# Feed-forward weights turned by the host: VectorE adds the raw tile to the low-rank product, ScalarE and GpSimd split it later

## The chip, the cores and the metric

The kernel runs on one core of a Trainium2 chip. The core has TensorE (PE in the rows), VectorE (DVE), ScalarE (ACT), GpSimd (POOL) and SyncE (SP), which issues the DMAs here. The metric is device microseconds of one execution. Three runs of the kernel before gave 982.81, 984.64 and 989.12 us; the median is 984.64 us.

## The reference

A layer on x of 2 x 1024 tokens of 512 features. LayerNorm of x feeds a causal attention with 32 heads of size 16 and 8 key groups, and a feed-forward block whose three weights each carry a low-rank term of rank 16. The result is x plus the product of the two:

```python
xn = _layernorm(x, axis=-1)
s = _L0_attn_ref(xn, Wq, Wkv, Wo, bo)
gate = xn @ gate_w.T + (xn @ gate_a.T) @ gate_b.T          # gate_w: 1376 x 512, gate_a: 16 x 512
up   = xn @ up_w.T   + (xn @ up_a.T)   @ up_b.T
hidden = silu(gate) * up
g = silu(hidden @ down_w.T + (hidden @ down_a.T) @ down_b.T)
return x + s * g
```

The kernel adds the low-rank product to the weight first (w + b a), once for each tile of 128 of the 1376 hidden features, and then multiplies.

## The kernel before

All float32 products are made of rounded parts: a tile is split in hi (ScalarE rounds it to float32r) and lo (the difference), and three matmuls hi·hi, hi·lo and lo·hi are summed in PSUM. So each weight tile goes through "fold" (sum of the weight and the low-rank product), "hi" and "lo" before its first use.

Two programs are interleaved on every engine. The **attention** walks through 640 slots: 16 rounds (batch x key group) of 40 slots, one head and key job in each. At even slots TensorE issues a pair of transposed score matmuls (`st`, two PSUM banks, one for each head); ScalarE makes `prob = exp(st)`, one head per slot. The next `st` pair waits until both exponentials of the pair before are done. TensorE also issues pairs of plain scores (`s`, three banks), which VectorE reduces to maxima (`part_max`), and every few slots the context matmuls (`o<-prob,v`) after GpSimd has masked the diagonal blocks. The maxima of half a round are negated, split (`neg_pad`, VectorE), transposed (`s<-ident,neg_pad`) and copied out (`neg_rows`, ScalarE).

The **background** is everything else, counted in steps (`STEPS`), and `interleave` gives about one step to each slot. Each engine has its own copy of the background, in which the same yields stand, so that an operation placed after some number of steps lands in a known slot. In order: LayerNorm and transposes of x, projections (`proj`), values, then for each of the NH = 11 tiles h of hidden features `hidden(h, c)` for four token chunks c of 8 steps each, one `proj` of 4 steps after c = 1, and the two folds (gate and up, 2 steps each) of tile h+1 also after c = 1. One h takes 40 steps, so a round. Then 11 down folds of 2 steps each, then `down(t)` and `out(t)` for 16 token tiles. The folds of tile 0 stand after the projection `AFTER[0]`, at the start of the attention; the down folds stand in slots 483 to 503, well before the attention's end.

A fold before: four TensorE transposes of the raw 128 x 512 tile (L909), four low-rank matmuls into the same bank (L913), ScalarE rounds the bank to `w_hi` (L1157), VectorE subtracts from the bank to get `w_lo` (L1392). A down fold: four transposes (L948), one low-rank matmul of 512 columns (L952), ScalarE `down_hi` (L1176), VectorE `down_lo` (L1412). The raw tiles come by DMA (L646) into `ring`, eight tiles of 2 KB per partition. `low_a`, the rounded factor a, is made once: ScalarE rounds it (L1144) after the values are stored, VectorE subtracts its lo rows (L1380), and both wait in line with what follows on their engine. GpSimd works on `hid` (L512, L514, L520) and on the masks (L503) in this phase.

## Time and profile before

| | us |
|---|---|
| runs: median (lowest, highest) | 984.64 (982.81, 989.12) |
| the profiled execution's own time | 989.02 |
| its span, first to last instruction | 987.3 |
| mean granted TensorE clock | 0.977 |
| PE, DVE, ACT, POOL busy | 927.0, 576.7, 487.5, 318.1 |

The profile is of one execution. An engine's busy share averages over stages with different limits, so a stretch has to be looked at by itself: which wait ends last there. In a timeline, PE rows with xN merge N matmuls; the start of the next row shows what a group really took, since matmuls overlap in the pipeline. "PEclk" 1.00 is 2.4 GHz and 0.50 is 1.2 GHz.

### The profile page before, as it was taken

How to read it: one execution, taken by the hardware profiler on the slowest of the kernel's cores; microseconds unless marked ns; L12 is line 12 of the kernel's file. 1: busy time of each engine (PE TensorE's matmuls, PEld its weight loads, DVE VectorE, ACT ScalarE, POOL GpSimd, SP SyncE). 2: the span in 40 equal slices, each digit the busy share in tenths (PEclk: the TensorE clock that was granted, in tenths of full speed). 3: DMA queues.
4: the chain of work that ended last, by engine and by line, in shares of the span. 5: the costliest groups of instructions: out<-in, count | busy, mean ns of one | idle time of the engine just before them, and what ended most of it. 6: DMA issues, size and time to landing. Idle time of an engine off the chain costs nothing.

```text
span 987.3 us, 18068 instructions
## 1 busy us (share of the span) xinstructions
PE 927.0 (94%) x6599; PEld 598.5 (61%) x6599; DVE 576.7 (58%) x1659; ACT 487.5 (49%) x978; POOL 318.1 (32%) x320
## 2 busy tenths in 40 slices
PE   2797999999999999999999999999999999999986
PEld 2665667676766676767676766554555555555764
DVE  6755666666666666666666666676566656530025
ACT  2432556565656565656565656555444434435211
POOL 4022234343535352525252525330213122120126
PEclk9899999999999999999999999989999999999998
DMA  9456242424242424242424243367565454534454
GB/s 293 132 186 206 64 136 80 133 83 134 82 134 83 133 83 125 86 124 88 119 89 124 93 127 101 101 186 195 166 169 146 124 158 122 139 105 135 144 150 150
DMA packets 142934, 129.02 MB, mean 131 GB/s; under 512 B 36176, under 2 KB 104368, under 8 KB 142624
## 3 DMA queue, kind: packets, MB, share of 16 engines
q1 hardware_dynamic: 142848, 127.87, 43.6%
q8 instruction: 54, 0.88, 0.4%
q14 instruction: 32, 0.26, 0.1%
HBM read 74.07 MB, written 53.22 MB: 129 GB/s over the span
## 4 chain that ended last, share of the span: by engine, by line
PE 84%; DVE 8%; ACT 3%; DMA 2%; issue 2%; POOL 0%; SPq 0%; POOLq 0%; DVEq 0%; ACTq 0%
PE bank L934 24%; PE o L1071 12%; PE bank L246 9%; PE s L1035 9%; PE st L1054 9%; PE bank L247 7%; PE bank L248 7%; DVE junk L1516 2%; PE bank L896 2%; DVE neg_pad L1532 1%; PE bank L909 1%; PE bank L913 1%; DVE hid L1406 1%; DMA inv_sums<-scratch_r 1%; ACT gate L1168 1%
## 5 line engine op out<-in xcount | busy, mean ns | idle before, releaser
L1297 ACT ACTIVATE prob<-st 128x512 f32<-128x512 f32 (+1 forms) x640 | 324.3, 554 | 287.7 <-PE st L1054 287.1
L1516 DVE CUSTOM_DVE_ANT_0 junk<-s,mask 128x128 bf16<-128x128 f32 (+3 forms) x512 | 229.3, 487 | 116.3 <-PE s L1035 115.5
L1519 DVE TENSOR_REDUCE part_max<-s 128x1 f32<-128x512 f32 x256 | 163.8, 681 | 103.9 <-PE s L1035 103.7
L503 POOL TENSOR_SCALAR_AFFINE_SELECT prob<-prob 128x512 f32<-128x512 f32 x128 | 82.3, 655 | 262.1 <-ACT prob L1297 261.6
L1035 PE MATMUL s<-k,q 64*128 64x512 f32 (+3 forms) x768 | 150.0, 379 | 10.5 <-DVE part_max L1516 8.5
L934 PE MATMUL bank<-x_hi,w_hi 64*128 64x512 f32 (+1 forms) x704 | 150.9, 415 | 2.4 <-DVE hid L1406 1.1
L1071 PE MATMUL o<-prob,v 128*32 128x512 f32 (+3 forms) x1536 | 145.3, 497 | 0.0
L934 PE MATMUL bank<-x_lo,w_hi 64*128 64x512 f32 (+1 forms) x704 | 142.9, 391 | 0.0
L934 PE MATMUL bank<-x_hi,w_lo 64*128 64x512 f32 (+1 forms) x704 | 142.2, 389 | 0.0
L1054 PE MATMUL st<-q,k 64*128 64x512 f32 (+3 forms) x768 | 137.2, 375 | 3.9 <-ACT prob L1297 3.8
L512 POOL TENSOR_TENSOR tanh<-tanh,hid 128x512 f32<-128x512 f32 (+1 forms) x44 | 56.5, 1285 | 166.4 <-DVE hid L1406 166.4
L1035 PEld LDWEIGHTS s<-k,q 64*128 64x128 f32 x768 | 77.3, 186 | 52.6 <-DVE part_max L1516 28.3
L1054 PEld LDWEIGHTS st<-q,k 64*128 64x128 f32 x768 | 72.0, 185 | 59.6 <-issue 35.5
L934 PEld LDWEIGHTS bank<-x_hi,w_hi 64*128 64x128 f32 (+1 forms) x704 | 68.7, 182 | 41.3 <-issue 30.6
L246 PE MATMUL bank<-down_hi,hid_in 128*128 128x512 f32 (+1 forms) x176 | 79.2, 450 | 3.0 <-issue 2.3
L520 POOL TENSOR_TENSOR hid_lo<-hid,tanh_hid_hi 128x512 fp32r<-128x512 f32 (+1 forms) x44 | 56.7, 1288 | 75.9 <-ACT tanh_hid_hi L1185 75.9
L1071 PEld LDWEIGHTS o<-prob,v 128*32 128x32 f32 x1536 | 39.7, 110 | 66.2 <-issue 62.3
L934 PEld LDWEIGHTS bank<-x_lo,w_hi 64*128 64x128 f32 (+1 forms) x704 | 69.0, 182 | 12.6
L934 PEld LDWEIGHTS bank<-x_hi,w_lo 64*128 64x128 f32 (+1 forms) x704 | 69.1, 183 | 7.4
L247 PE MATMUL bank<-down_lo,hid_in 128*128 128x512 f32 (+1 forms) x176 | 70.1, 399 | 0.0
L248 PE MATMUL bank<-down_hi,hid_in 128*128 128x512 f32 (+1 forms) x176 | 69.9, 397 | 0.0
L514 POOL TENSOR_TENSOR hid<-tanh,hid 128x512 f32<-128x512 f32 (+1 forms) x44 | 56.5, 1283 | 3.5
(121 smaller groups left out, 1014.6 us busy)
## 6 DMA issues: line engine op xcount, KB each, us to landing
hid_in<-scratch_hid SPq DMA_DIRECT2D x16, 1408.0 KB, 7.4
q<-scratch_q SPq DMA_DIRECT2D x60, 200.0 KB
scratch_hid<-tanh_hid_hi SPq DMA_DIRECT2D x40, 256.0 KB, 2.1
scratch_hid<-hid_lo SPq DMA_DIRECT2D x40, 256.0 KB, 2.4
scratch_o<-o_sb SPq DMA_DIRECT2D x32, 256.0 KB
scratch_q<-proj_hi SPq DMA_DIRECT2D x30, 256.0 KB
k<-scratch_k SPq DMA_DIRECT2D x30, 192.0 KB
ctx<-scratch_o SPq DMA_DIRECT2D x16, 256.0 KB, 3.9
```

Of the source, the lines that this page charges most:

```text
L246: pe.matmul(out, lhs_hi, rhs_hi, start=start, stop=False)
L247: pe.matmul(out, lhs_hi, rhs_lo, start=False, stop=False)
L248: return pe.matmul(out, lhs_lo, rhs_hi, start=False, stop=stop)
L503: ins = pool.affine_select(out=blk, in_=blk, compare_op=ALU.is_ge, fill=0.0, base=0, pattern=[[0, REP], [1, P]], channel_multiplier=-1)
L520: pool.tensor_tensor(hid_l[0:hp, n % 2], hid[0:hp, n % 2], hid_h[0:hp, n % 2], ALU.subtract)\
L934: mm = pe.matmul(bank[i][0:hp, :], w_[half, h % 2, i, kt, 0:hp], x_[half, c, kt], start=not cross and kt == 0 and w_ is wh and x_ is xh, s ...
L1035: pe.matmul(sb_[(p + odd) % S_BANKS][:, 0:wd], q[half, g % 2, h // 2, qt * P:(qt + 1) * P], k[half, g % 2, k0:k0 + wd], start=True, stop=T ...
L1054: mm = pe.matmul(st[odd][:, col:col + q1 - q0], k[half, i % 2, kt * P:(kt + 1) * P], q[half, i % 2, h // 2, q0:q1], start=True, stop=True)
L1071: mm = pe.matmul(ob[32 * h:32 * h + 2 * HD, q0 % C:q0 % C + q1 - q0], v[:, i % 3, kt].rearrange("p a e -> p (a e)"), prob[:, job % 3, h, c ...
L1297: nc.scalar.activation(prob[:, job % 3, h, 0:JOB_COLS[j]], st[at % ST_BANKS][:, 0:JOB_COLS[j]], ACT.Exp, scale=float(HD) ** -0.5).then_inc ...
L1516: ins = dve.tensor_tensor_reduce(junk[:, n % S_BANKS, 0:wd], bank_[:, 0:wd], mask[:, C - wd:C], 1.0, LOWEST, ALU.add, ALU.max, part[:, h, ...
L1519: ins = dve.tensor_reduce(part[:, h, qt, dst:dst + 1], bank_[:, 0:wd], AX.X, ALU.max)
```

## The change

The host lays gate_w and up_w out transposed, in tiles [h, p, k, 128] of 128 hidden features, and down_w transposed, so a raw tile lands in the form in which the product needs it. The transposes on TensorE go. The sum is made by VectorE: `ring = bank + ring` (PSUM and SBUF in, SBUF out). ScalarE rounds the sum from `ring` to `w_hi` or `down_hi`, and GpSimd subtracts (`w_lo`, `down_lo`) from `ring`. A fold keeps its 2 steps. The folds of tile 0 move ahead of `AFTER[0]`. Raw tiles are reloaded after GpSimd's subtraction, later in the order. `down(0)` waits for each `down_lo` when it needs it.

```diff
+    for i in range(2):
+        yield "fold", 0, i
     for c, blk in AFTER[:SOON]:
         yield "proj", c, blk
-    for i in range(2):
-        yield "fold", 0, i
...
-                        fold=(w_lo, 2 * a + b + 1), down_fold=(d_lo, a + 1), down=(y_done, a + 1),
+                        fold=(w_sum, 2 * a + b + 1), down_fold=(d_sum, a + 1), down=(y_done, a + 1),
...
+            def low_weight(h, i):
+                n = 2 * h + i
+                pool.wait_ge(w_hi, n + 1)
+                pool.tensor_tensor(wl[:, h % 2, i, :, 0:rows[h]], raw_tile(n), wh[:, h % 2, i, :, 0:rows[h]],
+                                   ALU.subtract).then_inc(w_lo, 1)
+
+            def low_down(h):
+                hp = rows[h]
+                pool.wait_ge(d_hi, h + 1)
+                if h == NH - 1:
+                    pool.wait_ge(d_lo, h)
+                pool.tensor_tensor(dl[0:hp, h], ring[0:hp, (RAW_DOWN + h) % 8], dh[0:hp, h], ALU.subtract).then_inc(d_lo, 1)
...
             def fold(h, i):
-                pe.wait_ge(raw_landed[n % 8], DMA * (n // 8 + 1))
                 pe.wait_ge(low_lo, 2)
                 out_ = take_bank(("fold", h, i))
                 for kt in range(KT):
-                    pe.matmul(out_[:, kt * P:kt * P + hp], ring[0:hp, n % 8, kt * P:(kt + 1) * P], ident[0:hp, 0:hp],
-                              is_transpose=True, start=kt == 0, stop=False, skip_group_check=True)
-                yield 1
-                for kt in range(KT):
                     mm = pe.matmul(out_[:, kt * P:kt * P + hp], a_gu[:, i, kt * P:(kt + 1) * P],
-                                   bT[:, i, h * P:h * P + hp], start=False, stop=kt == KT - 1, skip_group_check=True)
-                mm.then_inc(filled, 1)
-                yield 1
+                                   bT[:, i, h * P:h * P + hp], start=True, stop=True)
+                    if kt == KT - 1:
+                        mm.then_inc(filled, 1)
+                    if kt % 2:
+                        yield 1
...
             def split_down(h):
-                key = ("down_fold", h, 0)
-                wait_filled(act, key)
-                nc.scalar.activation(dh[0:rows[h], h], bank_of(key)[0:rows[h], :], ACT.Copy).then_inc(d_hi, 1)
+                hp = rows[h]
+                act.wait_ge(d_sum, h + 1)
+                nc.scalar.activation(dh[0:hp, h], ring[0:hp, (RAW_DOWN + h) % 8], ACT.Copy).then_inc(d_hi, 1)
...
+                yield 1
                 for h in range(NH):
                     yield STEPS["down_fold"]
                     split_down(h)
...
+            def add_down(h):
+                key, hp, n = ("down_fold", h, 0), rows[h], RAW_DOWN + h
+                dve.wait_ge(raw_landed[n % 8], DMA * (n // 8 + 1))
+                wait_filled(dve, key)
+                dve.tensor_tensor(ring[0:hp, n % 8], bank_of(key)[0:hp, :], ring[0:hp, n % 8], ALU.add).then_inc(d_sum, 1)
```

How it moves instructions, at three places. First TensorE at the folds of tile 1, in round 1 (`bank<-bT,low_a` is the low-rank product, `bank<-ident,ring` the transposes). Before:

```order
L909 MATMUL bank<-ident,ring 128x128 x3
L1035 MATMUL s<-k,q 128x512 [waits s_read]
L1035 MATMUL s<-k,q 128x512
L913 MATMUL bank<-bT,low_a 128x128 x4
L1054 MATMUL st<-q,k 128x512 [waits exp_done]
L1054 MATMUL st<-q,k 128x512
L1035 MATMUL s<-k,q 128x384 [waits s_read]
L1035 MATMUL s<-k,q 128x384
```

and now:

```order
L940 MATMUL bank<-bT,low_a 128x128 [waits up_read,gate_read,low_lo_done]
L940 MATMUL bank<-bT,low_a 128x128
L1057 MATMUL s<-k,q 128x512 [waits s_read]
L1057 MATMUL s<-k,q 128x512
L940 MATMUL bank<-bT,low_a 128x128 x2
L1076 MATMUL st<-q,k 128x512 [waits exp_done]
L1076 MATMUL st<-q,k 128x512
L1057 MATMUL s<-k,q 128x384 [waits s_read]
L1057 MATMUL s<-k,q 128x384
```

The transposes are gone, and of the four products two now stand ahead of the `s` pair and two behind it; `st` and `s` stand where they did.

Second, ScalarE at the start of the attention, just behind the rounding of `low_a`. Before:

```order
L1144 ACTIVATE low_a<-prob 96x1024 [waits xn_ready,v_stored1,v_stored0]
L1297 ACT_TABLE_LOAD [waits p_stored1,p_stored0]
L1297 ACTIVATE prob<-st 128x512 [waits st_done] x2
L1125 ACTIVATE proj_hi<-bank 128x512 [waits p_stored0,filled]
L1297 ACTIVATE prob<-st 128x512 [waits st_done] x2
```

and now:

```order
L1166 ACTIVATE low_a<-prob 96x1024 [waits xn_ready,v_stored1,v_stored0]
L1178 ACTIVATE w_hi<-ring 128x512 [waits w_sum]
L1319 ACT_TABLE_LOAD [waits p_stored1,p_stored0]
L1319 ACTIVATE prob<-st 128x512 [waits st_done] x2
L1178 ACTIVATE w_hi<-ring 128x512 [waits w_sum]
L1319 ACTIVATE prob<-st 128x512 [waits st_done] x2
```

The first `w_hi`, which waits for VectorE's first sum, now stands ahead of the table load and the first exponentials. On TensorE the first fold stands where the projection's first six matmuls stood, and waits for `low_lo`, the lo rows of `low_a`.

Third, ScalarE at the first down folds. Before (the two `prob` rows behind each `down_hi` are the two heads of one `st` pair):

```order
L1314 ACTIVATE o_sb<-o 128x512 [waits o_stored1,pv_done]
L1176 ACTIVATE down_hi<-bank 128x512 [waits filled]
L1297 ACTIVATE prob<-st 128x512 [waits pv_done,st_done]
L1297 ACTIVATE prob<-st 128x512 [waits st_done]
L1176 ACTIVATE down_hi<-bank 128x512 [waits filled]
L1185 ACTIVATE tanh_hid_hi<-hid 96x512 [waits hid_done]
```

and now:

```order
L1336 ACTIVATE o_sb<-o 128x512 [waits o_stored1,pv_done]
L1319 ACTIVATE prob<-st 128x512 [waits pv_done,st_done]
L1195 ACTIVATE down_hi<-ring 128x512 [waits d_sum]
L1204 ACTIVATE tanh_hid_hi<-hid 96x512 [waits hid_done]
L1319 ACTIVATE prob<-st 128x512 [waits st_done] x2
L1327 ACTIVATE neg_rows<-s 32x128 [waits m_landed1,m_turned]
```

`down_hi` has moved from ahead of a pair of exponentials to between its two halves, and waits for VectorE's sum. (In the last `x2` row, the first is the second head of the pair above, the second the first head of the next pair.) All eleven down folds stand so now.

## Rows read from the trace of the kernel before

**Rows 1.** The page, parts 1 and 4: busy time, the chain by engine

```profile
PE 927.0 (94%) x6599; PEld 598.5 (61%) x6599; DVE 576.7 (58%) x1659; ACT 487.5 (49%) x978; POOL 318.1 (32%) x320
...
PE 84%; DVE 8%; ACT 3%; DMA 2%; issue 2%; POOL 0%; SPq 0%; POOLq 0%; DVEq 0%; ACTq 0%
```

**Rows 2.** Windows: stretch and length; busy us (instructions) of PE, PEld, DVE, ACT, POOL; PEclk, DMA share, GB/s

```profile
230.00:560.00 330.00, 326.76 (x2761) 218.96 (x2761) 205.64 (x632) 191.04 (x391) 135.11 (x135) 1.00 0.36 108
...
660.00:665.00 5.00, 5.00 (x19) 2.72 (x17) 3.00 (x15) 2.28 (x4) 0.63 (x1) 0.50 0.89 296
```

**Rows 3.** Timeline, folds of tile 3: start us, us, engine, line, operation [idle before, releaser]

```profile
226.65 0.50 PE L1054 MATMUL st<-q,k 64*128 64x512 f32 x2
226.76 0.60 ACT L1157 ACTIVATE w_hi<-bank 128x512 fp32r<-128x512 f32 x1 [1.74 <-PE bank L913]
...
227.25 1.08 ACT L1297 ACTIVATE prob<-st 128x512 f32<-128x512 f32 x2
227.38 0.66 PE L909 MATMUL bank<-ident,ring 128*128 128x128 f32 x4
...
227.79 0.64 PE L913 MATMUL bank<-bT,low_a 96*128 96x128 f32 x4
228.00 0.55 DVE L1516 CUSTOM_DVE_ANT_0 junk<-s,mask 128x384 bf16<-128x384 f32 x1
228.39 0.50 PE L1054 MATMUL st<-q,k 64*128 64x512 f32 x2
```

**Rows 4.** Groups by line and form: busy us, mean ns of one, idle before

```profile
L909 PE MATMUL bank<-ident,ring 128*128 128x128 f32 x80 | 13.4, 291 | 0.0
...
L948 PE MATMUL bank<-ident,ring 128*128 128x128 f32 x40 | 7.6, 319 | 0.6 <-DVE hid L1406 0.6
...
L520 POOL TENSOR_TENSOR hid_lo<-hid,tanh_hid_hi 128x512 fp32r<-128x512 f32 x40 | 51.6, 1289 | 66.4 <-ACT tanh_hid_hi L1185 66.4
...
L1392 DVE TENSOR_TENSOR w_lo<-bank,w_hi 128x512 fp32r<-128x512 f32 x20 | 13.8, 691 | 1.3 <-ACT w_hi L1157 0.7
```

**Rows 5.** Timeline, the start of the attention

```profile
88.78 0.50 PE L246 MATMUL bank<-x_hi,wq_hi 128*128 128x512 f32 x1
...
90.35 0.50 PE L1054 MATMUL st<-q,k 64*128 64x512 f32 x2
...
93.51 1.06 ACT L1144 ACTIVATE low_a<-prob 96x1024 fp32r<-96x1024 f32 x1 [4.40 <-DMA scratch_v<-v_sb]
94.58 1.28 ACT L1297 ACT_TABLE_LOAD   x1
94.60 1.22 DVE L1380 TENSOR_TENSOR low_a<-prob,low_a 32x1024 fp32r<-32x1024 f32 x1 [5.88 <-ACT low_a L1144]
...
95.88 1.08 ACT L1297 ACTIVATE prob<-st 128x512 f32<-128x512 f32 x2
...
96.56 0.80 PE L1035 MATMUL s<-k,q 64*128 64x512 f32 x2 [5.71 <-DVE part_max L1516]
...
100.14 0.79 PE L1054 MATMUL st<-q,k 64*128 64x512 f32 x2
```

**Rows 6.** Timeline, the same start, the first hidden product's weight load (PEld)

```profile
106.02 0.18 PEld L934 LDWEIGHTS bank<-x_hi,w_hi 64*128 64x128 f32 x2 [0.84 <-DVE w_lo L1392]
```

**Rows 7.** Timeline, the down folds

```profile
650.77 0.50 PE L1054 MATMUL st<-q,k 64*128 64x384 f32 x4
...
651.34 1.27 POOL L514 TENSOR_TENSOR hid<-tanh,hid 96x512 f32<-96x512 f32 x1
651.37 1.08 ACT L1297 ACTIVATE prob<-st 128x512 f32<-128x512 f32 x2
651.51 1.13 DVE L1532 TENSOR_TENSOR neg_pad<-neg_max,neg_pad 128x16 fp32r<-128x16 f32 x1
...
652.50 0.50 PE L1054 MATMUL st<-q,k 64*128 64x384 f32 x4 [0.41 <-ACT prob L1297]
```

**Rows 8.** Line 1532 (ns min/median/max; first and last start us)

```profile
L1532 DVE TENSOR_TENSOR neg_pad<-neg_max,neg_pad x32: 174/176/1157, 63.4 to 876.1; 128x16 fp32r<-128x16 f32 x32
```

More of the change, by code:

```diff
@@ L550, in background @@
                 low_query_weights(3)
+                yield NUMBER_STEPS["fold", 0, 1] - done
+                done = NUMBER_STEPS["fold", 0, 1]
+                for i in range(2):
+                    low_weight(0, i)
                 for h in range(NH):
@@ L560, in background @@
                         finish(h, c)
-                yield 2 * STEPS["down_fold"]
+                        if c == 1 and h + 1 < NH:
+                            yield 3 * STEPS["fold"]
+                            low_weight(h + 1, 0)
+                            yield STEPS["proj"] - STEPS["fold"]
+                            low_weight(h + 1, 1)
+                            done += 2 * STEPS["fold"] + STEPS["proj"]
+                yield 4
+                low_down(0)
                 low_hidden(NH - 1, NCH - 1)
-                yield (NH - 2) * STEPS["down_fold"]
+                for h in range(1, NH):
+                    yield STEPS["down_fold"]
+                    low_down(h)
                 def add(t):
@@ L635, in load_raw @@
                 elif before >= 0:
-                    wait_filled(sp, ("fold", *divmod(before, 2)))
+                    sp.wait_ge(w_lo, before + 1)
                 if n < RAW_LOW:
                     h, i = divmod(n, 2)
-                    dst, src = ring[0:rows[h], n % 8], raw_weights[i][h * P:h * P + rows[h]]
+                    dst, src = raw_tile(n), raw_weights[i][h, :, :, 0:rows[h]]
                 elif n < RAW_DOWN:
@@ L715, in background @@
                     store_value(c)
+                yield 2 * STEPS["fold"]
                 for c, blk in AFTER[:SOON]:
@@ L718, in background @@
                     store_projection(c, blk)
-                for i in range(2):
-                    yield STEPS["fold"]
-                    load_more_raw(i)
                 for h in range(NH):
@@ L728, in background @@
                             load_more_raw(RAW_LOW + c)
+                        if h == 0 and c == 0 or h + 1 < NH and c == 2:
+                            for i in range(2):
+                                load_more_raw(2 * (h + c // 2) + i)
                         if c == 1:
-                            if h + 1 < NH:
-                                for i in range(2):
-                                    yield STEPS["fold"]
-                                    load_more_raw(2 * (h + 1) + i)
-                            yield STEPS["proj"]
+                            yield (2 * STEPS["fold"] if h + 1 < NH else 0) + STEPS["proj"]
                             store_projection(*AFTER[SOON + h])
@@ L993, in background @@
                     yield from value(c)
+                for i in range(2):
+                    yield from fold(0, i)
                 for c, blk in AFTER[:SOON]:
                     yield from project(c, blk)
-                for i in range(2):
-                    yield from fold(0, i)
                 for h in range(NH):
@@ L1153, in split_weight @@
             def split_weight(h, i):
-                key = ("fold", h, i)
-                hp = rows[h]
-                wait_filled(act, key)
-                nc.scalar.activation(wh[:, h % 2, i, :, 0:hp],
-                                     bank_of(key)[:, :].rearrange("p (k h) -> p k h", k=KT)[:, :, 0:hp],
-                                     ACT.Copy).then_inc(w_hi, 1)
+                n = 2 * h + i
+                act.wait_ge(w_sum, n + 1)
+                nc.scalar.activation(wh[:, h % 2, i, :, 0:rows[h]], raw_tile(n), ACT.Copy).then_inc(w_hi, 1)
             def read_gate(h, c):
@@ L1239, in background @@
                 split_low_a()
+                for i in range(2):
+                    yield STEPS["fold"]
+                    split_weight(0, i)
                 for c, blk in AFTER[:SOON]:
@@ L1242, in background @@
                     split_projection(c, blk)
-                for i in range(2):
-                    yield STEPS["fold"]
-                    split_weight(0, i)
                 for h in range(NH):
@@ L1463, in background @@
                 low_of_low(1, a_gu, a_raw, slice(BESIDE_ROWS, 2 * BESIDE_ROWS))
+                for i in range(2):
+                    yield STEPS["fold"]
+                    add_weight(0, i)
                 for c, blk in AFTER[:SOON]:
@@ L1466, in background @@
                     low_projection(c, blk)
-                for i in range(2):
-                    yield STEPS["fold"]
-                    low_weight(0, i)
                 for h in range(NH):
```

71 lines of the change are left out of this document (34 added, 37 removed).

## The prediction

> **What bounds the kernel now.** I read the page first. TensorE is busy 94% of the span, and the chain that ended last runs on it for 84% [rows 1]: look for the engine that is both fullest and on the chain. The windows then say where that holds: from 230 to 560 us TensorE is busy 326.76 of 330 us at the full clock, 2.4 GHz [rows 2]. So work taken from TensorE can shorten this kernel, if the next engine has room at the very place where the work is taken. The rest of my reading is of timelines at those places: the ten pairs of gate and up folds in the steady rounds (all alike, one in each round; [rows 3] show one), the folds of tile 0 at the start [rows 5, 6], and the eleven down folds [rows 7].
>
> **Removed from TensorE.** In one fold the transposes start at 227.38 and the low-rank products at 227.79: four transposes cost 0.41 us on the path, not the 0.66 us of the row [rows 3], which overlap. Twenty folds in the steady rounds: 20 x 0.41 = 8.2 us. Eleven down folds: 11 x 0.41 = 4.5 us at the full clock, and more where the clock stood at 0.50, 1.2 GHz, as it did from 660 to 665 us [rows 2]; the mean of L948 is 319 ns against 291 of L909 [rows 4]. I take 5.0 us. The folds of tile 0: about 1 us. Full credit: some 14 us. What follows asks how much of it the other engines let through.
>
> **Steady rounds, ten places.** First half: the transposes ahead of the `s` pair go and half the products move behind it, so `s` comes only 0.2 us sooner and the `st` pair of 226.65 0.41 us sooner. Second half: from `st` at 226.65 to `st` at 228.39 are 1.74 us, of which TensorE would now need 1.74 - 0.41 = 1.33. But `st` at 228.39 needs both exponentials of the pair before, and these ended at 227.25 + 1.08 = 228.33 [rows 3]. TensorE and ScalarE tie here. The matmul takes 0.50, the two exponentials 1.08 and the handover 0.06, so the interval can't fall under 1.64 us: at most 0.10 is gained of the second 0.41. `w_hi` leaves its place ahead of these exponentials, which is what makes even that 0.10 possible. VectorE then holds the next `s` pair: it needs the bank of the first maximum of 384 columns, at 228.00 + 0.55 [rows 3], which stands in an unbroken row of VectorE work that starts from the `s` pair between the first fold's two parts and so moves by 0.2 to 0.3 us only. TensorE issues in order, so that is what the whole round gains. I take 0.3 us for each place, **-3.0 us** in all; the ends are 0.2 (VectorE moves with `s` alone) and 0.5 (0.41 + 0.10).
>
> What hides the added work: GpSimd's subtraction costs 1.29 us by its twin L520 [rows 4]; the first use of the tile is some 14 slots on, so it lies beside the products of c = 2 and 3, and GpSimd's next masks are four slots behind the first subtraction. VectorE's sum replaces L1392, 0.69 us, and no longer waits for ScalarE. ScalarE's rounding stays one operation of about 0.6 us, now ahead of two pairs in which TensorE has a projection to do. These cost nothing here; without that cover GpSimd would bring 20 x 1.29 = 26 us. The reloads of raw tiles, later on SP's queue, are four tiles of h ahead and not felt.
>
> **Start, tile 0.** Before, TensorE did six matmuls of the projection and an `st` pair (88.78 to 90.35 + 0.50) ahead of its 5.71 us wait, and ScalarE loaded its table (1.28) while VectorE made the lo rows of `low_a`, done at 94.60 + 1.22 = 95.82; the first exponentials ran at 95.88 [rows 5]. Now TensorE's first fold waits for those lo rows, so the 2.1 us of work ahead of the wait moves behind it. And ScalarE's first `w_hi` waits for VectorE's first sum: lo rows 95.82, two maxima of 384 columns to about 96.95 (0.55 each [rows 3]), sum 0.69 [rows 4], `w_hi` 0.60, then the table load 1.28, exponentials at 99.5 instead of 95.88. They end at 100.6, and the second `st` pair follows at about 100.7, where it stood at 100.14 [rows 5], but with the whole projection (12 matmuls of 0.26, by 88.78 to 90.35: 3.1 us) still to do in place of the folds (four parts of 0.41 to 0.66, about 2.2 us) and a wait of 0.84 us for `w_lo` [rows 6]. To the first hidden product, at 106.02 before, 5.9 us behind that `st` pair: 100.7 + 5.9 - 3.0 + 3.1 = 106.7 at the full clock. TensorE has two idle gaps instead of one, though, and after the one gap its matmuls ran at the lower level (0.79 us for an `st` pair at 100.14 against 0.50 at 90.35 [rows 5]), so part of the projection will take up to twice as long. I take **+1.5 us**, between 0 and +3.
>
> **Down folds.** Credit 5.0 us, as above. Against it stands ScalarE's order: `down_hi` sits between the two exponentials of each of the eleven pairs and waits for the sum. The chain of a pair becomes 0.50 (`st`) + 0.54 + 0.60 (`down_hi`) + 0.54 + 0.06 = 2.24 us, where the pair of 650.77 took 1.73 and already waited 0.41 us for the exponential [rows 7]. So 0.5 us more wherever TensorE has less to do than that; where a group of context matmuls stands in the pair, nothing. I count five such pairs besides the first: 2.5 us. The first pair is worse. VectorE's `neg_pad`, 0.176 us in the median [rows 8], took 1.13 at 651.51, until GpSimd's L514 ended at 652.61 [rows 7], and the first sum is next in VectorE's line: 652.64 + 0.69 = 653.3, then `down_hi` 0.6, `tanh_hid_hi` 0.6, second exponential 0.6: 655.1, where `st` stood at 652.50. That is 2.6 us, with all of TensorE's line behind it. Sum: -5.0 + 2.5 + 2.6 = **+0.1 us**. The ends: -5 (ScalarE never late) and +6 (0.5 on all ten other pairs, 2.6, and some 3 us of matmuls slowed by a lower clock that lasts through the stretch, less the credit and rounded). The four `wo_hi` behind it also sit in mid-pair: 2.24 us of chain against about as much TensorE work (six matmuls of 0.26 and two pairs of scores at about 0.35): +0.3. GpSimd's eleven `down_lo` take 14.2 us of a stretch of 30; `down(0)` waits for them one by one and is not held by the last of them.
>
> **Sum.** -3.0 + 1.5 + 0.1 + 0.3 = -1.1 us against the profiled execution's 989.02 (span 987.3 and 1.7 around it), so 987.9. That execution was 4.4 us above the median of the three, 984.64; off the median the forecast is **983.5 us**.
>
> **A rule weighed.** GpSimd held up VectorE's `neg_pad`, which reads two SBUF tiles (1.13 us against 0.176 [rows 7, 8]), yet L1392, which reads PSUM and SBUF, has a mean of 691 ns, that of the other VectorE operations on 512 columns, and was not held up [rows 4]. The Trainium skill, SBUF — State Buffer, section "Who interferes with whom", says that a VectorE instruction with two SBUF inputs and a GpSimd instruction that reads SBUF exclude each other for their whole length. By that rule the new sums (one PSUM input) are safe but 42 us more of GpSimd subtraction are added that can lock others out; the trace agrees on both kinds.
>
> **Rivals.**
> - *Full credit* (chance 0.12): ScalarE and VectorE overlap more than I read and TensorE's 14 us come off whole: 984.6 - 14 = 971. For it: TensorE is 99% busy in the rounds. Against: `st` at 228.39 came 0.06 us behind the exponentials [rows 3].
> - *Only the ends are better than I think* (0.10): the down folds give their 5, the start nothing: 984.6 - 3 - 5 = 976.5.
> - *GpSimd locks out VectorE* (0.10): the two `neg_pad`, the casts ahead of them and the four `wo_lo` near the down folds read SBUF alone; half of the eight meet a subtraction and lose 1.0 us each, the excess of 651.51 [rows 7, 8]: 983.5 + 4 = 987.5. Against it: the subtractions in the rounds stand at slots where no `neg_pad` is.
> - *Slower* (0.11): ScalarE's wait for the sum in mid-pair. One mechanism: sum late behind maxima, `down_hi` late, second exponential late, `st` late, `s` late, maxima late again, in all eleven pairs. By the first pair's loss, 2.6 us, on six of eleven and 0.5 on the rest: 18 us, less 5, plus the start's 1.5, less 3: 984.6 + 11.6 = 996. It is slower by over 1% once the mean pair loses 1.5 us; TensorE, idle in between, would then also stay at the lower level.
>
> **Chances and range.** My forecast has 0.57. About 1% (9.8 us) is what a measurement here can tell from no change. Faster by over 1%: 0.13 (full credit and a sliver of the second rival). Slower: 0.11. Within: 0.76. The range, 975.5 to 991.5, takes in the bounds of the three terms (-5 to -2, 0 to +3, -5 to +6, not all at once), the second and third rivals, and leaves out full credit and the slower case.
>
> **What would show it.** Right: an `st` interval of 1.64 to 1.70 us at the second fold of each round, with the wait on `prob`; each round shorter by about 0.3 us; the first exponentials at about 99.5 us, behind the table load; a wait of 2 to 3 us of `st` for `prob` at the first down fold and `st` intervals of at least 2.2 us after it. Wrong: rounds shorter by 0.8 us (then ScalarE did not bind), `w_hi` waiting long for its sum in the rounds, masks late behind GpSimd's subtractions, TensorE's clock down at the folds of the steady rounds, or a stretch of down folds under 27 us.

## The result, and the profile after

The changed kernel takes **1004.9 us** (median of 6 runs, 1003.76 to 1009.23), the kernel before, measured beside it, 986.64 (6 runs): a ratio of 1.0194, 95% interval 1.0168 to 1.0219. The prediction was 983.5 within 975.5 to 991.5. It is slower by 1.9%, and outside the range.

The profiled execution took 1004.8 us, 15.7 more in its span than the one of before (1003.0 against 987.3). The page of the changed kernel, busy time and the chain by engine:

```profile
PE 929.2 (93%) x6467; PEld 591.6 (59%) x6467; DVE 575.6 (57%) x1659; ACT 489.4 (49%) x978; POOL 359.6 (36%) x353
...
PE 78%; DVE 8%; DMA 5%; ACT 5%; issue 2%; SPq 2%; POOL 0%; POOLq 0%; DVEq 0%; ACTq 0%
```

Read the two numbers of TensorE together: 132 instructions fewer than in [rows 1], yet 2.2 us more of busy time. That points to a lower clock (mean granted clock 0.957, before 0.977), and the windows show where. Windows of the changed kernel, at the folds of four steady rounds and at the down folds (columns as in [rows 2]; the third from the end is the granted clock):

```profile
130.00:136.00 6.00, 5.87 (x22) 3.35 (x20) 4.13 (x10) 3.38 (x7) 3.24 (x3) 0.72 0.13 38
180.00:186.00 6.00, 5.80 (x22) 3.44 (x20) 4.63 (x10) 3.27 (x6) 3.85 (x4) 0.74 0.22 71
230.00:236.00 6.00, 5.79 (x28) 3.73 (x24) 4.70 (x12) 3.29 (x7) 4.23 (x4) 0.84 0.35 110
280.00:286.00 6.00, 5.79 (x36) 3.17 (x27) 5.12 (x15) 4.11 (x8) 3.91 (x4) 1.00 0.42 126
...
660.00:690.00 30.00, 20.94 (x95) 8.98 (x98) 19.48 (x61) 16.50 (x34) 16.35 (x17) 0.63 0.66 194
```

TensorE is nearly always busy at the folds in all four, but in three its clock is partly at the lower level, 1.2 GHz. It falls so in six of the ten steady rounds, the first three and the seventh to ninth; before it stood at 1.00 from 230 to 560 us [rows 2]. What that costs is seen in the projection's matmuls right behind the fold (changed kernel, round of 132 us):

```profile
132.73 0.79 PE L246 MATMUL bank<-x_hi,wq_hi 128*128 128x512 f32 x1
133.32 0.63 PE L247 MATMUL bank<-x_lo,wq_hi 128*128 128x512 f32 x1
133.75 0.63 PE L248 MATMUL bank<-x_hi,wq_lo 128*128 128x512 f32 x1
```

0.63 us each here, and 0.43 from the second start to the third. In the round without a drop at 285 us the same matmuls take 0.40, with 0.24 between their starts.

**Where the time went.** A round is measured from one turned `neg_pad` (`s<-ident,neg_pad` on TensorE, every second one) to the next; the first stands at the end of the start.

| stretch | before | after | difference |
|---|---|---|---|
| start, to the first turned `neg_pad` | 104.81 | 107.41 | +2.6 |
| ten steady rounds | 495.5 | 501.7 | +6.2 |
| the two rounds that hold the down folds | 52.75 + 56.59 | 55.61 + 60.08 | +6.4 |
| the rest | 277.7 | 278.3 | +0.6 |

Of the ten rounds, four took 49.2 to 49.3 us, **less** than the 49.5 of before, and six 50.6 to 50.8.

**The fold.** One fold pair of the kernel before, ahead of and between the rows of [rows 3], TensorE only:

```profile
223.19 1.92 PE L1071 MATMUL o<-prob,v 128*32 128x512 f32 x16
...
225.04 0.66 PE L909 MATMUL bank<-ident,ring 128*128 128x128 f32 x4
225.63 0.50 PE L1035 MATMUL s<-k,q 64*128 64x512 f32 x2
226.06 0.66 PE L913 MATMUL bank<-bT,low_a 96*128 96x128 f32 x4
...
227.00 0.44 PE L1035 MATMUL s<-k,q 64*128 64x384 f32 x2
```

The same place in the changed kernel, in a round without a drop of the clock:

```profile
279.01 1.92 PE L1093 MATMUL o<-prob,v 128*32 128x512 f32 x16
...
280.86 0.44 PE L940 MATMUL bank<-bT,low_a 96*128 96x128 f32 x2
281.23 0.49 PE L1057 MATMUL s<-k,q 64*128 64x512 f32 x2
281.65 0.44 PE L940 MATMUL bank<-bT,low_a 96*128 96x128 f32 x2
...
281.76 1.29 DVE L1539 TENSOR_REDUCE part_max<-s 128x1 f32<-128x512 f32 x2 [0.88 <-PE s L1057]
282.02 0.50 PE L1076 MATMUL st<-q,k 64*128 64x512 f32 x2
...
282.60 0.44 PE L1057 MATMUL s<-k,q 64*128 64x384 f32 x2
...
283.69 0.50 PE L1076 MATMUL st<-q,k 64*128 64x512 f32 x2
```

From one `s` pair to the next both take 1.37 us: that is VectorE's two maxima of 0.68 each, behind which the score bank is free. Before, TensorE filled these 1.37 us: `s` 0.43, four products 0.59, `st` 0.35. Now half of the products stand ahead of `s`, and TensorE starts the second `s` 0.23 us later than the 0.35 that an `st` pair takes with work right behind it. That is how gaps are reckoned here: from start to start, less what the group before takes when the next one follows at once. By it there are two more gaps in this fold pair, 0.14 us ahead of the `st` at 283.69 and 0.22 ahead of the `s` at 284.26, so 0.59 us in all.

**The start.** Changed kernel:

```profile
94.85 1.22 DVE L1402 TENSOR_TENSOR low_a<-prob,low_a 32x1024 fp32r<-32x1024 f32 x1 [6.81 <-ACT low_a L1166]
...
96.12 1.12 PE L940 MATMUL bank<-bT,low_a 96*128 96x128 f32 x4 [7.94 <-DVE low_a L1402]
...
98.07 0.63 ACT L1178 ACTIVATE w_hi<-ring 128x512 fp32r<-128x512 f32 x1 [3.25 <-DVE ring L1414]
98.72 1.28 ACT L1319 ACT_TABLE_LOAD   x1
100.01 1.08 ACT L1319 ACTIVATE prob<-st 128x512 f32<-128x512 f32 x2
...
101.15 0.80 PE L1076 MATMUL st<-q,k 64*128 64x512 f32 x2 [1.72 <-ACT prob L1319]
...
108.62 0.51 PE L963 MATMUL bank<-x_hi,w_hi 64*128 64x512 f32 x2
```

`w_hi`, table load, exponentials, `st`: the order that the prediction laid out against [rows 5], with the first exponentials at 100.0 (99.5 predicted) and the first hidden product 2.6 us later than in [rows 6].

**The first down fold.** Changed kernel:

```profile
660.11 1.26 POOL L524 TENSOR_TENSOR hid<-tanh,hid 96x512 f32<-96x512 f32 x1
660.29 1.12 DVE L1552 TENSOR_TENSOR neg_pad<-neg_max,neg_pad 128x16 fp32r<-128x16 f32 x1
661.33 1.28 DVE L1432 TENSOR_TENSOR ring<-bank,ring 128x512 f32<-128x512 f32 x2
...
662.04 0.63 ACT L1195 ACTIVATE down_hi<-ring 128x512 fp32r<-128x512 f32 x1 [1.61 <-DVE ring L1432]
662.58 0.61 ACT L1204 ACTIVATE tanh_hid_hi<-hid 96x512 fp32r<-96x512 f32 x1
...
663.10 0.57 ACT L1319 ACTIVATE prob<-st 128x512 f32<-128x512 f32 x1
663.73 0.80 PE L1076 MATMUL st<-q,k 64*128 64x384 f32 x4 [3.48 <-ACT prob L1319]
```

Again the predicted chain, with a wait of 3.5 us where 2 to 3 were named. Behind it TensorE's clock is down for some 22 of 30 us (0.63 in the window above). The kernel before had it down here too, but for less of the stretch, some 8 of 30 us:

```profile
660.00:690.00 30.00, 28.49 (x158) 14.61 (x157) 21.10 (x59) 17.29 (x33) 1.27 (x2) 0.86 0.72 206
```

### The profile page after: what moved, and what is told of

The parts are those of the page before. It is cut to its first block, busy times and chain, and to the rows that moved or that the text cites. A ratio compares the mean times of both kernels' runs of the same rounds, so it can differ in the third digit from the quotient of the medians.

```text
span 1003.0 us, 17849 instructions
## 1 busy us (share of the span) xinstructions
PE 929.2 (93%) x6467; PEld 591.6 (59%) x6467; DVE 575.6 (57%) x1659; ACT 489.4 (49%) x978; POOL 359.6 (36%) x353
## 4 chain that ended last, share of the span: by engine, by line
PE 78%; DVE 8%; DMA 5%; ACT 5%; issue 2%; SPq 2%; POOL 0%; POOLq 0%; DVEq 0%; ACTq 0%
PE bank L963 24%; PE o L1093 12%; PE st L1076 9%; PE s L1057 9%; PE bank L246 9%; PE bank L247 6%; PE bank L248 6%; ACT prob L1319 2%; DVE junk L1536 2%; DVE neg_pad L1552 1%; SPq L654 1%; DVE hid L1426 1%; PE bank L940 1%; DMA inv_sums<-scratch_r 1%; PE bank L929 1%
## 5 line engine op out<-in xcount | busy, mean ns | idle before, releaser
L1076 PE MATMUL st<-q,k 64*128 64x512 f32 (+3 forms) x768 | 139.4, 381 | 12.9 <-ACT prob L1319 12.0
L522 POOL TENSOR_TENSOR tanh<-tanh,hid 128x512 f32<-128x512 f32 (+1 forms) x44 | 56.5, 1284 | 166.1 <-DVE hid L1426 166.1
L524 POOL TENSOR_TENSOR hid<-tanh,hid 128x512 f32<-128x512 f32 (+1 forms) x44 | 56.5, 1283 | 3.5
```

The source lines that it names most:

```text
L1076: mm = pe.matmul(st[odd][:, col:col + q1 - q0], k[half, i % 2, kt * P:(kt + 1) * P], q[half, i % 2, h // 2, q0:q1], start=True, stop=True)
```

## Experiments

Two theories at first. **Work**: without the transposes TensorE has too little in the fold steps, and its granted clock falls behind them. **Chain**: the longer way over VectorE, ScalarE and GpSimd costs the time, and the clock only shows it. Later a third, **layout**: which side of the `s` pair the short matmuls stand on. The expectations speak of sixteen gate and up folds, eight down folds and 64 transposes; there are 22, 11 and 88, and each edit was made in all of them. Diffs are against the changed kernel unless another is named.

| kernel | median us (runs) | first `neg_pad` | ten rounds | drops | two rounds with down folds |
|---|---|---|---|---|---|
| e1_products_twice | 1006.88 (4) | 109.80 | 501.7 | 4 | 55.6 + 60.6 |
| e2_ident_transposes | 999.49 (4) | 109.04 | 495.3 | 0 | 55.3 + 60.1 |
| e3_before_no_transposes | 981.62 (10) | 105.33 | 494.6 | 2 | 52.8 + 54.1 |
| e4_start | 1001.27 (4) | 104.85 | 501.8 | 6 | 55.6 + 60.6 |
| e5_down_pairs | 998.85 (4) | 107.55 | 501.6 | 6 | 52.8 + 59.1 |
| e6_down_ident | 1002.44 (4) | 108.16 | 501.8 | 6 | 55.3 + 59.0 |
| e7_all_four | 987.78 (8) | 107.66 | 495.1 | 0 | 52.6 + 53.2 |
| e9_apart | 986.98 (12) | 104.70 | 495.5 | 0 | 52.7 + 53.7 |
| e10_together | 981.43 (6) | 105.35 | 489.4 | 0 | 52.7 + 53.5 |
| e11_fill_steady | 986.54 (12) | 108.36 | 495.1 | 0 | 52.7 + 53.2 |
| e12_layout_alone | 993.14 (7) | 107.61 | 489.1 | 0 | 55.6 + 60.3 |
| e13_products_first | 1000.99 (4) | 106.51 | 508.6 | 9 | 52.7 + 53.2 |
| e14_no_idle | 985.12 (10) | 104.82 | 490.7 | 1 | 52.5 + 57.8 |
| e15_down_second | 983.94 (10) | 106.45 | 489.1 | 0 | 52.7 + 56.5 |

The kernel before lay at 984.5 to 985.7 beside these, and at 986.6 beside the changed one, so up to 2 us between medians that were measured at different times are not the edit's. A drop is a steady round with the granted clock down behind its folds (its length is then some 1.5 us over that of its neighbours). Rounds and drops are of the one profiled execution of each kernel. Kernels with the same TensorE order at the folds can be taken together, though: the changed one, e4, e5 and e6 have 24 drops in 40 rounds; e10, e12, e14 and e15 have 1 in 40; the kernel before, e2, e7 and e11, with transposes in the folds, have none in 40.

### Work or chain: e1, e2, e3

```
e1: + four products (the fold's own) in step 1, all four products in step 2
e2: + 4 x pe.transpose(out_[:, kt * P:(kt + 1) * P], ident[:, :], ident[:, :]) in step 1, all four products in step 2
e3, against before:
-   pe.matmul(out_[...], ring[0:hp, n % 8, ...], ident[0:hp, 0:hp], is_transpose=True, ...)   # gate and up folds
```

> The changed kernel, with the four low-rank products of each of the sixteen gate and up folds issued twice: a first set in the fold's first step, the set that is used in its second, so that TensorE has as many instructions in each fold step as the kernel before had. The down folds stay light. Clock theory (TensorE's granted clock falls to its lower level behind the lightened folds, in six of the ten steady rounds, at about 1.5 us each): the granted clock stays at 1.00 through the steady rounds, a round is about 49.5 us instead of 50.8, and the kernel is 6 to 9 us faster than the changed one, 996 to 999. Chain theory (the time goes to the longer chain VectorE, ScalarE, GpSimd and its waits, the clock is a symptom): eight more products in each pair of folds only add work, the six long rounds stay at about 50.8 or grow by 0.5, the kernel takes 1005 to 1010.

> The changed kernel, with four transposes of the identity in each gate and up fold's first step, into the bank that the products then overwrite: the kernel before's count and kind of TensorE instructions, but with nothing in them that is waited for. Clock theory, if transposes keep the clock up as the matmuls do: steady rounds at a granted clock of 1.00 and about 49.5 us, 996 to 999. If it is the matmuls alone that keep it up, some rounds still fall to the lower level and the time lies at 1000 to 1006, apart from the kernel with doubled products. Chain theory: 1005 to 1010.

> The kernel before, with the transposes of its sixteen gate and up folds left out and nothing else: ScalarE and VectorE still make hi and lo from the bank, so the raw gate and up weights are missing from the result. Clock theory: taking TensorE's work out is enough to lose its clock; the granted clock falls to the lower level behind the folds in several of the ten steady rounds, each such round is about 1 us longer than the others, and the kernel is no faster than before, 984 to 993. Chain theory: without the longer chain the removed 64 transposes are a plain gain, the clock stays at 1.00 in the steady rounds, each round is 0.3 to 0.8 us shorter than 49.5, 976 to 983.

e2 gave what the work theory said: ten rounds back at 49.5 us and full clock, 5.4 us off the median. But its edit does two things: it adds the idle transposes and it moves two products from ahead of the `s` pair to behind it, so it does not single out the work (e12 below does the second alone). e3, which leaves the raw gate and up weights out of the result, gave two drops in the kernel before, with not one link of the new chain in it, so the chain is no precondition of a drop. (Its first round is long as well, 50.73 us, because the start's lower clock lasts until 109 us there.) But its rounds without a drop took 48.93 us, and it was 0.35% faster than before (0.9965, interval 0.9935 to 0.9995): the drops are the work theory's, the time and the round are what the chain theory named. And e1 was a miss for the work theory: it has as many matmuls as before and still four drops. TensorE was busy without a gap before one of them (windows of e1):

```profile
280.00:284.00 4.00, 4.00 (x34) 2.18 (x22) 2.89 (x8) 1.83 (x5) 2.55 (x2) 1.00 0.68 193
284.00:289.00 5.00, 5.00 (x21) 3.19 (x19) 3.08 (x8) 2.68 (x6) 2.55 (x2) 0.66 0.05 10
```

### Start and down folds: e4, e5, e6, and all together: e7

```
e4:   for i in range(2):
-         yield STEPS["fold"]
+         yield STEPS["fold"] * (2 - i)       # ScalarE, first fold pair
          split_weight(0, i)
      ...
-         yield STEPS["proj"]
+         yield STEPS["proj"] - STEPS["fold"]
e5: - yield 1      + yield 2                  # ScalarE, ahead of the down folds; one less behind them
e6: + 4 x pe.transpose(out_[...], ident[:, :], ident[:, :]) in step 1 of each down fold
e7: e2 + e4 + e5 + e6
```

> The changed kernel, with ScalarE's two hi copies of the first fold pair moved behind the table load and the first exponentials (two fold steps for the first copy instead of one). Order theory for the start (the hidden projection starts 2.6 us later than before because the copy of hi stands ahead of ScalarE's table load, so the first exponentials and with them the second pair of score matmuls come late): first exponentials at about 98.7 instead of 100.0, the first hidden matmul at 106.5 to 107.5 instead of 108.6, the kernel 1 to 2 us faster, 1003 to 1004. Against it, that the start is late by TensorE's wait for VectorE's low half alone (7.9 us in both orders) and by the lower clock at 100 to 104: the first hidden matmul stays at 108 to 109 and the time at 1005.

> The changed kernel, with ScalarE's hi copies of the down weights one step later, so that each stands between two pairs of exponentials and not inside one. Chain theory for the down folds (the stretch of the two rounds with down folds is 6.4 us longer than before because ScalarE waits for VectorE's sum inside a pair and the score matmuls wait for ScalarE, 3.5 us at the first): the rounds of 55.6 and 60.1 us shrink to about 54 and 57, the wait of 3.5 us goes, the kernel is 3 to 6 us faster than the changed one. Clock theory (the removed transposes leave TensorE too light there, and its granted clock falls whatever ScalarE's order): the granted clock stays at its lower level for most of 660 to 690, and the two rounds lose less than 1.5 us.

> The changed kernel, with four transposes of the identity in the first step of each of the eight down folds, into the bank that the product then overwrites (the gate and up folds stay light). Clock theory for the down folds: the granted clock is back at its upper level for most of 660 to 690, and the rounds of 55.6 and 60.1 us come to 53 to 54 and 56 to 57.5, 5 to 6 us less. Chain theory: the wait of 3.5 us on the exponential and the long steps stay, the clock falls in that wait all the same, and the two rounds stay within 1 us.

> The changed kernel with all four edits together: transposes of the identity in the gate and up folds and in the down folds, the first hi copies behind the first exponentials, the down weights' hi copies between pairs of exponentials. If start (about 2.6 us), clock in the steady rounds (about 8) and down folds (about 6 to 9) are the whole difference and add up: 984 to 989, no slower than before by more than 0.5%. If something else of the change costs as well (VectorE's three-input additions, GpSimd's subtractions beside the other engines): 990 or more.

In e4 the exponentials come at 96.7 and nothing waits behind them:

```profile
96.73 1.08 ACT L1319 ACTIVATE prob<-st 128x512 f32<-128x512 f32 x2 [1.88 <-PE st L1076]
...
98.10 0.79 PE L1076 MATMUL st<-q,k 64*128 64x512 f32 x2
...
106.07 0.50 PE L963 MATMUL bank<-x_hi,w_hi 64*128 64x512 f32 x2
```

The first hidden product is at 106.07, as before (106.02), and the median 3.6 us lower. For the size of the start's share I would not trust one profile: the first `neg_pad` of the eight kernels of the table with this edit lies at 104.7 to 108.4, mean 106.1, of the six others of the new chain (the changed one among them) at 107.4 to 109.8, mean 108.3. So the edit is worth about 2.2 us.

e5 takes the waits on the exponentials away. Waits in the stretch of the down folds, the changed kernel and then e5 (us in total, times, longest):

```profile
PE st L1076 <- ACT prob L1319: 8.0, 7, 3.5
```

```profile
PE st L1076 <- ACT prob L1319: 2.6, 5, 0.7
```

The first of the two rounds falls by 2.8 us, the second by only 1.0, with the clock still down; and e6 alone brings 0.3 and 1.1. Each theory expected one of the two edits to do nearly all of it. e5's 3.8 us lie in the 3 to 6 that the chain theory gave it, but the clock stayed down as the work theory said; e6's 1.4 fall short of the work theory's 5 to 6. Together (e7) they bring 3.0 and 6.9, 9.9 us against 5.2 for the two apart: the clock is down in the second round as long as either the waits or the light folds are there. This is read from two rounds of one execution of each kernel, but it repeats: the five kernels with both edits (e7, e9, e10, e11, e13) have a second round of 53.2 to 53.7 us, the three with e5's alone 56.5 to 59.1, e6 59.0, and the five with neither 60.1 to 60.6. The medians of whole executions can't show it: by their ratios to before, the four edits apart bring 1.4% in sum and 1.7% together, and the intervals are about as wide as that difference. e7's stretch at the full clock:

```profile
650.00:670.00 20.00, 18.21 (x135) 10.15 (x132) 17.46 (x56) 14.86 (x32) 13.97 (x14) 1.00 0.58 180
670.00:690.00 20.00, 18.94 (x108) 10.24 (x108) 12.58 (x32) 11.95 (x23) 6.75 (x6) 1.00 0.69 189
```

e7 takes 987.78 us, ratio 1.0021 to before (0.9996 to 1.0047). It keeps every addition of VectorE and every subtraction of GpSimd that the change brought, so the loss lay nearly whole in the start's order, TensorE's order and clock at the folds, and the down folds. By itself e7 is a weak test of the additions and subtractions: its down folds run at the full clock and take 3.5 us less than before's, which could hide a cost elsewhere. Two kernels below are a sharper one. e3 has the old chain and e10 and e12 the new one, all with the same TensorE order at the gate and up folds, and their rounds without a drop take 48.93 us (e3, e12) and 48.94 (e10).

### Fewer steps, and where the products stand: e8 to e11

```
e8:  e4 and - fold=2, down_fold=2   + fold=1, down_fold=2;   MIDDLE = SLOTS * N - 14;
     SyncE also waits for the last hidden tile before it loads wo
e9:  e4 + e5 + e6, and in the steady rounds:  - fold, fold, projection   + fold, projection, fold
e10: e4 + e5 + e6, and in every gate and up fold:
-    products 0, 1; yield 1; products 2, 3; yield 1
+    yield 1; products 0, 1, 2, 3; yield 1
e11: e7 without the transposes of the identity in the folds of tile 0
```

> The changed kernel with the first hi copies behind the first exponentials, and each gate and up fold's four products in one step instead of two, so that no step of TensorE has only two short products in it beside a pair of score matmuls (14 background steps fewer under the attention's slots). Clock theory: with the light steps gone the clock has nothing to fall behind: full granted clock in most of the ten steady rounds, at about 48.9 to 49.3 us each, 993 to 999 in all. Chain theory: sum, hi and lo are pressed into half the steps, so the chain of three engines is felt more: steady rounds over 50 us, 1001 or more.

e8 took 1093.88 us (4 runs) and says nothing on the question. Twenty folds lie in the steady rounds, so by the program's own count 20 steps had to come off the attention's and not 14. Its rounds take 54 to 61 us, and TensorE waits for VectorE at the hidden tiles (waits of e8):

```profile
PE bank L962 <- DVE hid L1425: 38.3, 28, 2.0
```

> The changed kernel with the first hi copies behind the first exponentials, the down weights' hi copies between pairs, transposes of the identity in the down folds only, and in the steady rounds the projection block put between the two folds of a pair (fold, projection, fold), so that the light steps are never more than two in a row; no idle work in the gate and up folds. Clock theory: most steady rounds keep a granted clock of 1.00 at 49.0 to 49.3 us each, nothing is paid for it, and the kernel takes 981 to 986, as fast as before or a little faster. Against it (it is the work in the fold steps that counts, not how they lie together): six rounds or so still fall to the lower level and the kernel takes 991 to 996.

> The changed kernel with the same three edits for start and down folds, and each gate and up fold's four products all in its second step, the first left to the attention alone; no idle work in the gate and up folds. Clock theory, by how evenly the work lies: steps with 0, 4, 0, 4 products are more uneven than 2, 2, 2, 2, so at least as many steady rounds (six of ten) fall to the lower level, 990 to 996. Against it, from the kernel before without its transposes, which had this layout and rounds of 48.93 us with two or three drops: 983 to 989.

> The kernel with all four edits, but without the transposes of the identity in the first pair of folds, where TensorE stands on the start's path at the lower clock. If the start of that kernel (first turned maxima at 107.7 against 104.9 in the one with only ScalarE's copies moved) is late by that work: 104.9 to 105.5 there, 984 to 986 in all, equal to the kernel before. If it is late for another reason: it stays at 107 to 108 and at 987 to 988.

e9 has the full clock but rounds of 49.55 us and gains nothing; its second fold stands alone, and TensorE waits there for `prob` (0.41 us at 282.27). e11's first `neg_pad` came at 108.36, not 105: the filler was not what made e7's start late. e10 refutes the work theory for the gate and up folds, and my expectation with it. With no idle transposes in them it has **no drop in ten rounds**, and rounds of 48.94. Its fold pair:

```profile
271.57 1.92 PE L1095 MATMUL o<-prob,v 128*32 128x512 f32 x16
...
273.43 0.50 PE L1059 MATMUL s<-k,q 64*128 64x512 f32 x2
273.86 0.66 PE L941 MATMUL bank<-bT,low_a 96*128 96x128 f32 x4
...
274.45 0.49 PE L1078 MATMUL st<-q,k 64*128 64x512 f32 x2
274.80 0.44 PE L1059 MATMUL s<-k,q 64*128 64x384 f32 x2
...
276.12 0.50 PE L1078 MATMUL st<-q,k 64*128 64x512 f32 x2 [0.28 <-ACT prob L1321]
```

Nothing stands ahead of `s`, and VectorE's 1.37 us are filled without a gap. TensorE does idle, though, further on: 0.28 us by the row, 0.36 by the starts, ahead of the `st` pair of the second fold, where it waits for the exponentials. That is the tie with ScalarE which the prediction named.

### Layout alone, and the down folds: e12 to e15

```
e12: the changed kernel with e10's order of the products alone
e13: e10 with  products 0, 1, 2, 3; yield 2
e14: e10 without e6's idle transposes
e15: e14 with the down fold's one product in step 2
```

> The changed kernel with one edit alone: each gate and up fold's four products together in its second step, instead of two in each. Layout theory (it is the alternation of two short products, score matmuls, two short products that costs TensorE 0.35 us a pair of folds and leaves the gaps behind which the clock falls): ten rounds at 48.9 to 49.0 us with no or few drops, about 10 us less than the changed kernel, 993 to 996. Work theory (too little work in the fold steps, whatever the layout; the kernel with start and down folds edited too owes its full clock to something else): still four or more rounds with a drop at over 50 us, 999 or more.

> The kernel with start and down folds edited and each gate and up fold's four products together, but in the fold's first step, the second left empty. Layout theory, by whether the products are together: as with the products in the second step, 48.9 to 49.0 a round, 980 to 983. If it matters that they stand right ahead of VectorE's addition (in the second step), or that the first step's score matmuls are not held back: rounds of 49.3 or more, or drops, 985 to 995.

> The kernel with the four products together in the second step, the first hi copies behind the first exponentials and the down weights' hi copies between pairs, and no idle transposes anywhere. Work theory for the down folds (one product in two steps is too little for TensorE's clock): the granted clock falls for much of 660 to 690 as with the pairs edit alone, the second of the two rounds with down folds takes 56 to 59 us instead of 53.5, 983 to 988 in all. Against it, if the idle transposes only cost: 52.7 and 53.0 in the two rounds, 979 to 981.

> The same without idle transposes, but each down fold's single product in its second step instead of the first. If the layout of the steps counts in the down folds as it does in the gate and up folds: the second round with down folds takes 53 to 54 us and the clock stays up, 979 to 982. If it is the work that counts there: no difference from the kernel with the product in the first step, within 1.5 us.

e12 shows that the order of the products is enough in the steady rounds: one edit, the same instructions, 11.8 us off the median, ten rounds of 489.1 us in all instead of 501.7, no drop. Against it, e2's idle transposes gain nothing there and cost 0.6 us a round. e13 is the counterpart: the four products together, but ahead of `s`. Nine drops, and the longest gap, 0.64 us by the row and 0.68 by the starts:

```profile
279.36 0.66 PE L940 MATMUL bank<-bT,low_a 96*128 96x128 f32 x4
279.95 0.50 PE L1058 MATMUL s<-k,q 64*128 64x512 f32 x2
280.29 0.40 PE L1077 MATMUL st<-q,k 64*128 64x512 f32 x2
...
281.32 0.44 PE L1058 MATMUL s<-k,q 64*128 64x384 f32 x2 [0.64 <-DVE part_max L1540]
```

Five kernels side by side, rounds without a drop, gaps by the starts:

| | ahead of the first `s` | behind it | gap ahead of the next `s` | all gaps of the fold pair | round | drops |
|---|---|---|---|---|---|---|
| e10, e12 | nothing | 4 products | none | 0.36 | 48.94, 48.93 | 0 |
| after | 2 products, 0.37 | 2 products | 0.23 | 0.59 | 49.30 | 6 |
| before | 4 transposes, 0.59 | 4 products | none | none | 49.53 | 0 |
| e13 | 4 products, 0.59 | nothing | 0.68 | 1.03 | 49.57 (one round) | 9 |

The round grows by what stands ahead of `s` (0.36 for 0.37, 0.59 and 0.63 for 0.59). The drops go with the gaps in these five, but not by a rule that holds for all: see the end of the next section. In the down folds the idle transposes do count: e14's second round takes 57.8 us against e10's 53.5 (granted clock 0.83 against 1.00 from 645 to 695 us), and where the product stands matters less (e15: 1.3 us in that round; 1.2 in the median, with intervals that overlap).

e10 beats both kernels: 981.43 us, ratio to before 0.9963 (0.9949 to 0.9978), 2.3% under the changed one. That is a small gain for a long way.

## Why the prediction was wrong

Its readings of waits held in the main; its assumption about the clock did not.

- **Steady rounds, -3.0 forecast, +6.2 measured.** The mechanism was right: `s` comes 0.22 us sooner behind the `o` matmuls (2.44 us before, 225.63 less 223.19; 2.22 after), VectorE then holds the next `s`, and the `st` interval at the second fold is 1.67 us, inside the 1.64 to 1.70 named. A round without a drop is 0.23 us shorter, by 0.3 forecast. **The step that failed** is the one that was never made: I took the full clock of [rows 2] as given, though the text listed "TensorE's clock down at the folds of the steady rounds" as what would show it wrong. Six drops of 1.5 us each are 9 us; less the 2.3 gained, that is the 6.2 measured, within 0.5.
- **"Half the products move behind it"** was seen from the wrong side. Before, all four stood behind `s`; the change moves half of them ahead of it. The 0.2 us that I named for `s` are right (0.59 less 0.37), but I didn't see the 0.37 as a price. The four products behind `s` lay in an interval that VectorE sets, so they had been free; ahead of it, two of them cost 0.37 us a round and left the gap. I also took 0.41 us for each four transposes. Those ahead of `s` took 0.59 (225.04 to 225.63), and this credit was really there: e12's ten rounds are 6.4 us shorter than before's. The four of the second fold gave nothing, because the `st` pair waits for `prob` there, as the text said.
- **Start, +1.5 forecast, +2.6 in the profile.** Right in mechanism, a little small, inside its ends. The order on ScalarE accounts for about 2.2 of it, by the comparison of fourteen kernels.
- **Down folds, +0.1 forecast, +6.4 measured**, just over the upper end of +6. The first wait was 3.5 us and not 2.6. The rest is mostly the clock again: down for some 22 of 30 us where it was down for some 8 before. The upper end had 3 us for it; e7 against e5, the two rounds at the full clock against the lower, gives 6.1. That the waits had to go as well as the light folds is what only both edits together showed.
- **The four `wo_hi`, +0.3**: the rest of the span grew by 0.6 us, but it lies anywhere from 274.8 to 279.3 in the kernels of the table, so this is no test.
- **GpSimd locks out VectorE** did not happen beyond what was there. `neg_pad` took 1.12 us at 660.29 beside GpSimd's L524, as at 651.51 before [rows 7], and TensorE waits for it 10 times in the steady rounds in both kernels, 3.7 us in all before and 3.4 after, by the list of its waits. The new sums, one input in PSUM, kept their 0.68 us:

```profile
L1414 DVE TENSOR_TENSOR ring<-bank,ring 128x512 f32<-128x512 f32 x20 | 13.7, 684 | 0.2 <-PE bank L940 0.2
```

- **The rival *Slower*** came to 996 by 18 us lost in the eleven pairs of the down folds, 1.6 a pair. The 6.4 us and the lost credit of 5 are 1.0 a pair. It had the lower clock in its last clause, and only for the down folds.

What stays open is the rule by which the clock falls. The gaps order four layouts (none, 0.36, 0.59 and 1.03 us in a fold pair: 0, 0, 6 and 9 drops in ten rounds), but that is no rule: e1 has four drops with no gap, e3 has two drops with the TensorE order of e12, and e9 has none with the same two products ahead of `s` as the changed kernel. Nor is the layout all that decides: the changed kernel issues the same instructions in each round and falls in the first three and the seventh to ninth only, e1 in the first, fourth, seventh and tenth. When in time the folds come may decide too, and no run moved them in time alone. The Trainium skill, TensorE: Matmul & The Clock Gate, section "A second HAM failure mode: psum-queue depth-cycling", tells of a kernel in which TensorE idles briefly and often between groups of matmuls and its clock swings between the two levels. The changed kernel looks like that, six swings with short gaps in each fold pair; but e12 has such gaps and no swing, and e1 swings without one. What no run tried either is other work of the same size in the fold steps of e1 and e3.

## What to carry to other kernels

Where two engines hand a buffer back and forth, find the interval that the other engine sets, and keep the short work inside it: in this kernel the same four matmuls cost nothing behind the score pair and 0.6 us a round ahead of it. A change that thins out TensorE must be costed at both clock levels, even where the trace of before shows the full clock in all steady rounds; and another order of the same instructions is worth a run before the change is given up. And edits that each remove one of two causes of a low clock are to be tried together: in the down folds 0.3 + 1.1 and 2.8 + 1.0 us apart became 9.9.

## What the runs showed of the hardware

- The granted clock fell to the lower level in rounds in which TensorE was busy 5.79 to 5.87 of the 6 us around the folds, and in e1 behind 4.00 of 4.00 us. It came back within the same round; each fall cost about 1.5 us.
- With nothing but another order of the same products in the gate and up folds (e12 against the changed kernel) the drops in the steady rounds went from six to none; over all kernels with these two orders, from 24 in 40 rounds to 1 in 40.
- GpSimd's 33 more subtractions, 41.5 us by the page of the profile (359.6 against 318.1 busy), cost no time that shows: a round without a drop takes 48.93 us without them (e3) and with them (e12).
